# Attention with a mixture of experts on one core: eight of nine expert turns written out with constant counts, one spare block, and the first row numbers loaded ahead of the waits

## The chip, the cores and the metric

The kernel runs on one core of one Trainium2 chip. Its time is the device time of one execution in microseconds. A profile is one further execution under the hardware profiler; its times are read from the start of its span.

## What is computed

One layer: linear attention with a residual, then a mixture of 16 experts of which each token takes two, with a residual. There are 16 x 256 = 4096 tokens of 128 numbers. An expert keeps no more than 640 tokens of each choice; later ones are dropped.

```python
    x = x + _L0_attn_ref(_layernorm(x, axis=-1), L0_attn_W_qkv, L0_attn_W_out, L0_attn_b_out)
    # attention: q = relu(q) + EPS; k = relu(k) + EPS; kv = k^T v; z = 1 / (q . sum(k) + EPS)
    #            out = (q kv z) W_out^T + b_out, by batch of 256 tokens
    # experts:
    logits = xf @ router_w
    probs = jax.nn.softmax(logits, axis=-1)
    w, idx = lax.top_k(probs, K)                       # K = 2 of E = 16
    ...
    keep = myrank < capacity                           # 640
    ...
    gate = jnp.einsum('ecd,edh->ech', xe, gate_w)
    up = jnp.einsum('ecd,edh->ech', xe, up_w)
    hidden = jax.nn.silu(gate) * up
    out = jnp.einsum('ech,ehd->ecd', hidden, down_w)
    out = out * wbuf[:, :, None]
    combined = jnp.zeros((T + 1, D), dtype=xf.dtype).at[dispatch.reshape(-1)].add(out.reshape(-1, D))
```

## The kernel before, in words

The program is written by hand for five engines, with a semaphore for every hand-over. It has three phases.

**Attention phase.** 16 steps, one for a batch of 256 tokens, each cut into stages that run with a lag against each other. For each step POOL takes a power (L350) for the layer norm and then issues four indirect DMAs (L366): each scatters 128 token rows (128 numbers, the expert's mark and the token's number, 528 bytes) from `xf` into the HBM buffer `xbuf` (in the profile: expert_rows), where each expert has a region of `PITCH` rows. The last three steps have no power before their scatters, since the powers run three steps ahead of the routing. At the start SP writes `SPARES` = 14 blocks of empty rows behind the experts' regions (L286), then zeroes `y2` (in the profile: expert_results). At the end of the phase SP, ACT and POOL write a block of empty rows (`tailrows`) behind each expert's last row (`write_tails`: seven, seven and two), and DVE and PE work out three tables: how many turns there will be (`turns_i`), the row at which each block begins (`row_i`), and each block's expert (`exp_i`, `eblk`).

**Expert phase.** A block is 128 rows of one expert. A turn is `U` = 8 blocks. The number of turns is known only on the chip; in the profiled execution it is 9, so 72 blocks. Each block goes through the engines so: SP loads its rows into `xe` (L305); PE transposes them (L922), ACT copies the result to `xeT` (L485); DVE copies the expert's weights to `ew` (L770) and makes the rows' targets `dst` (L780); PE multiplies gate and up (L931), ACT takes silu (L491), DVE the product `hT` (L787), PE multiplies down (L940), ACT copies to `ye` (L499), and POOL scatters the rows of `ye` into `y2` by an indirect DMA (L392). `xe`, `ew`, `ye` and `dst` have eight buffers each, so a buffer is used again one turn later; `xeT`, `sg`, `hT` have two.

PE, DVE and SP have turn 0 written out and ACT turns 0 and 1; the turns behind are a loop on each engine (`Fori`), POOL's loop has all of them. In a loop the counts to wait for are registers, worked out anew each turn (`counts_of`, `done_of`, L253), and a wait for a register's value stands beside an increment of a dummy semaphore `b_held`. At the start of each turn SP and DVE load the turn's eight row numbers and expert numbers into registers (`table_of`, L245). SP's order at the start of the phase: wait for `rows`, load `turns`, wait for the spares, all tails and all scatters (`d_spare`, `d_tail`, `d_ptail`, `d_sc`), load eight row numbers, issue eight loads of `xe`.

**Final phase.** When POOL's last scatter has landed (`d_ye`, then `y_all`), SP and ACT load the results (`yg`), DVE, ACT and POOL weight them and add them to `xa`, and SP writes the output.

The names and lines that the change touches are `sizes` (L7), SP's `load_turn` (L298), POOL's loop (L386), ACT's (L516), DVE's `turn` (L790) with `row_i` (L759), and PE's loop (L949).

Of the kernel before, what the change touches and what calls it, by code (L numbers as in the profile page):

```python
# [6 lines left out]
def sizes(tokens, experts, choices):  # L7

    cap = -(-tokens * choices * 5 // (experts * 4))
    blk = 128  # L10
    maxb = -(-choices * cap // blk)
    pitch = maxb * blk + blk
    per_turn = 8
    minturns = 3


    spares = max(per_turn - 1, minturns * per_turn - choices * cap // blk)
    return cap, blk, maxb, pitch, per_turn, minturns, spares


def linear_attention_moe(nc, x, w_qkv, w_out, b_out, router_w, gate_w, up_w, down_w,
# [13 lines left out]
    P = 128  # L35
# [5 lines left out]
    CAP, BLK, MAXB, PITCH, U, MINTURNS, SPARES = sizes(NB * N, E, K)  # L41
    SPARE = E * PITCH
    DROPPED = SPARE + SPARES * BLK
    MAXN = K * NB * N // BLK + E
    MAXN += -MAXN % U
    NTOK = NB * N
    W = D + 4
# [6 lines left out]
    with ExitStack() as ctx:  # L54
# [141 lines left out]
        NS = 4  # L196
# [45 lines left out]
        def table_of(eng, tab, i, last):  # L242

            at = tab[0:1, U * i:U * i + U] if isinstance(i, int) else tab[0:1, bass.ds(U * i, U)]
            return nc.values_load_multi_w_load_instructions(  # L245
                at, engines=[eng.engine], min_val=0, max_val=last,
                skip_runtime_bounds_check_because="DVE makes the table from the experts' numbers and PITCH")[1]
# [23 lines left out]
        def _(sp):  # L271
# [18 lines left out]
            sp.wait_ge(T["rows"], 1)  # L290
            turns = sp.value_load(turns_i[0:1, 0:1], min_val=0, max_val=MAXN // U - MINTURNS) + MINTURNS
            sp.wait_ge(d_spare, 16 * SPARES)
            sp.wait_ge(d_tail, 16 * POOLT)
# [3 lines left out]

            def load_turn(i, counts):  # L298
                rows = table_of(sp, row_i, i, DROPPED - BLK)
                for u in range(U):  # L300
                    done_of(sp, "xeT_ps", counts, u, U)
                    if not isinstance(i, int):
                        sp.sem_inc(b_held, 1)
                    done_of(sp, "dst", counts, u, U)
                    sp.dma_start(xe[:, u, :], xbuf[bass.ds(rows[u], BLK), :]).then_inc(d_xe[u], 16)  # L305

            load_turn(0, counts_of(sp, 0))
            with sp.Fori(1, turns) as i:
                load_turn(i, counts_of(sp, i, range(-U // NS, 0)))

# [10 lines left out]
        def _(pool):  # L321
# [63 lines left out]

            with pool.Fori(0, turns) as i:  # L386
                counts = counts_of(pool, i, range(U // NS))
                for u in range(U):

                    done_of(pool, "ye", counts, u, 0)  # L390
                    pool.sem_inc(b_held, 1)
                    nc.gpsimd.indirect_dma_start(  # L392
                        out=y2, out_offset=bass.IndirectOffsetOnAxis(ap=dst[:, u:u + 1], axis=0),
                        in_=ye[:, u, :], in_offset=None,
                        bounds_check=K * NTOK - 1, oob_is_err=False).then_inc(d_ye[u], 16)
            for u in range(U):
                pool.wait_ge(d_ye[u], 16 * turns)
                pool.sem_inc(b_held, 1)
# [10 lines left out]
        def _(act):  # L409
# [105 lines left out]
            turn(counts_of(act, 1), 16, None)  # L515
            with act.Fori(2, turns) as i:  # L516
                turn(counts_of(act, i), act.snap(16 * i), act.snap(16 * i - 16))
# [17 lines left out]
        def _(dve):  # L535
# [222 lines left out]
            dve.wait_ge(T["rows_ps"], 1)  # L758
            nc.vector.tensor_copy(row_i[:, :], banks[5][0:1, P:2 * P]).then_inc(T["rows"], 1)  # L759
            nc.vector.tensor_copy(exp_i[:, :], banks[5][0:1, 0:P])  # L760
# [29 lines left out]
            def turn(i, counts, landed, scattered):  # L790
                experts = table_of(dve, exp_i, i, E)
                of_turn = eblk[:, 0:U] if isinstance(i, int) else eblk[:, bass.ds(U * i, U)]
                nc.vector.tensor_copy(eturn[:, :], of_turn).then_inc(b_eturn, 1)
                for u in range(U):
                    weights(counts, u, experts[u])
                    if u == 0:
                        dve.wait_ge(b_eturn, i + 1)
                        dve.sem_inc(b_held, 1)
                    targets(counts, u, landed, scattered)
                    if u >= 1 or not isinstance(i, int):  # L800
                        hidden(counts, u)

            dve.wait_ge(d_ew, 48)
            turn(0, counts_of(dve, 0), 16, None)
            with dve.Fori(1, turns) as i:
                turn(i, counts_of(dve, i, range(-U // NS, U // NS)), dve.snap(16 * i + 16), dve.snap(16 * i))
# [13 lines left out]
        def _(pe):  # L820
# [122 lines left out]
            for u in range(U):  # L943
# [3 lines left out]
                if u >= 2:  # L947
                    down(counts, u)
            with pe.Fori(1, turns) as i:  # L949
                counts, landed = counts_of(pe, i), pe.snap(16 * i + 16)  # L950
                for u in range(U):
                    transpose_in(counts, u, landed)
                    gate_up(counts, u)
                    down(counts, u)
            last = counts_of(pe, turns, range(-1, 0))
            gate_up(last, 0)
# [32 lines left out]
```

## Time and profile before

| | us |
|---|---|
| median of three runs without a profile | 262.67 |
| lowest and highest | 262.15, 263.38 |
| span of the profiled execution | 303.2 |
| attention phase's scatters in it, first to last start | 37.8 to 140.3 |
| expert phase's scatters in it, first to last start | 152.3 to 272.8 |

The profiled execution has no time of its own beside its span. The span runs from the first instruction recorded to the last, and is 40.5 us longer than the median of the runs that carry no profile. So a duration of one instruction can be taken from it, but a stretch of the span cannot be set equal to a stretch of the timed run without asking what the waits in it are. In the rows, the first two columns of a time line or a chain are the start and the duration in us; brackets hold the engine's idle time before the instruction and what ended it; a row of a source line gives count, durations in ns (least, median, most) and the first and last start.

### The profile page before, as it was taken

Reading aid. Unit: us, or ns where it says so; the run is one execution under the profiler, and the core shown is the slowest. Engines: PE = TensorE matmul, PEld = TensorE weight load, DVE = VectorE, ACT = ScalarE, POOL = GpSimd, SP = SyncE. Lnnn points to the kernel's source line nnn. Section 1 sums busy time; section 2 is a strip of 40 time slices with the busy share of each in tenths; the row PEclk is TensorE's granted clock in tenths of the full one; section 3 lists DMA queues with packets and bytes.
Section 4 is the critical chain, followed back from the end, with each engine's and each line's share of the span. In section 5 each row is a group of like instructions: output and inputs, shape, how many; then the busy total and the mean of one; then the engine's idle time right before and its main releaser. Section 6 shows DMA issues by size and latency. Waiting matters only on the chain.

```text
span 303.2 us, 5241 instructions
## 1 busy us (share of the span) xinstructions
PE 181.9 (60%) x1016; PEld 153.2 (51%) x1016; DVE 172.2 (57%) x985; ACT 126.0 (42%) x448; POOL 174.4 (58%) x200
## 2 busy tenths in 40 slices
PE   6684969877764765401569585866877576640000
PEld 5574848666553754301458474755766465530000
DVE  5987766567485657762345364454546354510892
ACT  2663865557574643220244233443435333420330
POOL 4775388585758757866056565556565565651360
PEclk9588995688999795555596879598779897965555
DMA  7997941010101111115332222222232222105992
GB/s 212 294 287 220 291 151 50 27 53 28 47 31 51 37 38 37 54 55 170 81 99 80 74 74 74 67 69 78 67 88 79 64 81 61 40 27 151 290 318 81
DMA packets 46148, 31.62 MB, mean 104 GB/s; under 512 B 4589, under 2 KB 42483, under 8 KB 46130
## 3 DMA queue, kind: packets, MB, share of 16 engines
q1 hardware_dynamic: 36482, 20.20, 25.0%
q0 software_dynamic: 4416, 8.67, 8.5%
q10 hardware_dynamic: 5232, 2.57, 3.3%
q14 instruction: 13, 0.11, 0.1%
q8 instruction: 5, 0.08, 0.1%
HBM read 14.57 MB, written 17.36 MB: 105 GB/s over the span
## 4 chain that ended last, share of the span: by engine, by line
issue 42%; PE 18%; another core or an unknown queue 13%; SPq 10%; DMA 5%; ACT 4%; DVE 4%; ACTq 1%; POOL 0%; POOLq 0%; DVEq 0%
PE bank L931 12%; PE bank L940 4%; DMA yg<-expert_results 3%; SPq L286 3%; PE bank L922 2%; ACT xeT L485 2%; DVE ysum L267 2%; DVE xa L267 2%; ACT ye L499 1%; SPq L240 1%; SPq L281 1%; SPq L280 1%; SPq L278 1%; ACT sg L491 1%
## 5 line engine op out<-in xcount | busy, mean ns | idle before, releaser
L392 POOL DMA_INDIRECT expert_results<-ye,dst x72 | 70.5, 979 | 60.8 <-ACT ye L499 39.7
L366 POOL DMA_INDIRECT expert_rows<-xf,slots x64 | 63.4, 990 | 25.0 <-issue 17.4
L931 PE MATMUL bank<-xeT,ew 128*128 128x128 f32 x288 | 57.6, 333 | 13.7 <-ACT xeT L485 9.9
L931 PEld LDWEIGHTS bank<-xeT,ew 128*128 128x128 f32 x288 | 47.8, 236 | 20.1 <-ACT xeT L485 13.1
L940 PE MATMUL bank<-ew,hT 128*128 128x128 f32 x144 | 37.7, 350 | 20.3 <-issue 14.4
L787 DVE TENSOR_TENSOR hT<-sg,bank 128x128 f32<-128x128 f32 x72 | 20.6, 286 | 51.4 <-ACT sg L491 32.7
L491 ACT ACTIVATE sg<-bank 128x128 f32<-128x128 f32 x72 | 20.1, 279 | 48.8 <-remote 23.3
L940 PEld LDWEIGHTS bank<-ew,hT 128*128 128x128 f32 x144 | 27.0, 234 | 25.0 <-issue 16.8
L499 ACT ACTIVATE ye<-bank 128x128 f32<-128x128 f32 x72 | 20.1, 280 | 22.1 <-remote 15.1
L770 DVE COPY ew<-ew_sb 128x384 f32 x72 | 27.9, 387 | 1.3 <-issue 1.3
L922 PE MATMUL bank<-ident,xe 128*128 128x128 f32 x72 | 23.5, 327 | 7.4 <-DMA xe<-expert_rows 7.1
L485 ACT ACTIVATE xeT<-bank 128x128 f32<-128x128 f32 x72 | 20.1, 280 | 18.4 <-PE bank L922 16.5
L350 POOL TENSOR_TENSOR rs<-ve,minus_half 128x2 f32<-128x2 f32 x16 | 12.2, 763 | 13.8 <-DVE ve L617 13.6
L848 PE MATMUL bank<-ident,xf 128*128 128x128 f32 x32 | 8.7, 366 | 18.0 <-ACT xf L452 16.8
L888 PE MATMUL bank<-gs,qk 128*128 128x129 f32 x64 | 12.6, 326 | 8.1 <-ACT gs L419 5.8
L922 PEld LDWEIGHTS bank<-ident,xe 128*128 128x128 f32 x72 | 12.2, 170 | 9.2 <-DMA xe<-expert_rows 7.7
L452 ACT ACTIVATE xf<-xa,nb,rs 128x128 f32<-128x128 f32 x32 | 13.9, 484 | 4.4 <-DVE nb L579 4.4
L888 PEld LDWEIGHTS bank<-gs,qk 128*128 128x128 f32 x64 | 9.7, 217 | 11.2 <-ACT gs L419 8.0
L267 DVE SCALAR_TENSOR_TENSOR ysum<-yg,wts,xa 128x128 f32<-128x128 f32 x24 | 9.3, 421 | 10.5 <-DMA yg<-expert_results 10.5
L419 ACT ACTIVATE gs<-bank 128x129 f32<-128x129 f32 (+1 forms) x32 | 8.7, 273 | 14.7 <-remote 8.0
L848 PEld LDWEIGHTS bank<-ident,xf 128*128 128x128 f32 x32 | 4.5, 176 | 20.4 <-ACT xf L452 18.9
L860 PE MATMUL bank<-wkT,xnT 128*128 128x128 f32 x64 | 14.2, 359 | 0.7 <-ACT xnT L419 0.7
(140 smaller groups left out, 400.1 us busy)
## 6 DMA issues: line engine op xcount, KB each, us to landing
xe<-expert_rows SPq DMA_DIRECT2D x72, 66.0 KB
expert_results<-zeros SPq DMA_DIRECT2D x1, 4096.0 KB
xs<-in_L_attn_x_dram SPq DMA_DIRECT2D x4, 512.0 KB, 5.3
yg<-expert_results SPq DMA_DIRECT2D x8, 256.0 KB, 8.6
yg<-expert_results ACTq DMA_DIRECT2D x8, 256.0 KB, 9.8
out_dram<-xa SPq DMA_DIRECT2D x8, 256.0 KB, 4.9
expert_rows<-tailrows SPq DMA_DIRECT2D x21, 66.0 KB, 3.3
expert_results<-ye,dst POOLq DMA_INDIRECT x72
```

The source lines that it names most:

```text
L267: nc.vector.scalar_tensor_tensor(out=(ysum if k == 0 else xa)[:, j, :], in0=yg[:, k, j, :], scalar=wts[:, j, k:k + 1], in1=(xa if k == 0 e ...
L366: nc.gpsimd.indirect_dma_start(out=xbuf, out_offset=bass.IndirectOffsetOnAxis(ap=slots[:, col:col + 1], axis=0), in_=xf[:, g % R, j, :], i ...
L392: nc.gpsimd.indirect_dma_start(out=y2, out_offset=bass.IndirectOffsetOnAxis(ap=dst[:, u:u + 1], axis=0), in_=ye[:, u, :], in_offset=None, ...
L485: nc.scalar.activation(xeT[:, u % 2, :], banks[u % 2][:, 0:P], ACT.Copy).then_inc(B["xeT"][u % NS], 1)
L491: nc.scalar.activation(sg[:, v % 2, :], banks[2 + v % 2][:, 0:P], ACT.Silu).then_inc(B["sg"][v % NS], 1)
L499: nc.scalar.activation(ye[:, v, :], banks[4 + v % 2][:, 0:D], ACT.Copy).then_inc(B["ye"][v % NS], 1)
L770: nc.vector.tensor_copy(ew[:, u, :], ew_sb[:, bass.ds(e, 1), :].rearrange("p o h -> p (o h)")).then_inc(B["ew"][u % NS], 1)
L787: nc.vector.tensor_tensor(hT[:, v % 2, :], sg[:, v % 2, :], banks[2 + v % 2][:, P:2 * P], ALU.mult).then_inc(B["hT"][v % NS], 1)
L888: ins = mm(banks[4][:, j * (D + 1):(j + 1) * (D + 1)], qk[:, q % R, j * P:(j + 1) * P], gs[:, q % R, D:], start=True, stop=True)
L922: nc.tensor.transpose(banks[u % 2][:, 0:P], xe[:, u, 0:D], ident[:, :]).then_inc(B["xeT_ps"][u % NS], 1)
L931: ins = mm(banks[2 + v % 2][:, c * P:(c + 1) * P], ew[:, v, c * D:(c + 1) * D], xeT[:, v % 2, :], start=True, stop=True)
L940: mm(banks[4 + v % 2][:, 0:D], hT[:, v % 2, :], ew[:, v, 2 * D:], start=True, stop=True).then_inc(B["y_ps"][v % NS], 1)
```

## The change

Every engine now has turns 0 to 7 written out (`STATIC` = 8), with constants in its waits, and a loop for the turns from 8 on. `MINTURNS`, the least number of turns, becomes 4096 x 2 / 1024 + 1 = 9. `b_held` is incremented in loops only. One spare block is written in place of 14; row numbers of blocks past the last one are cut to `SPARE` by a minimum in the instruction that fills `row_i`, so all such blocks read that one. SP's register load of turn 0's row numbers moves ahead of its waits.

```diff
-    minturns = 3
-    spares = max(per_turn - 1, minturns * per_turn - choices * cap // blk)
+    minturns = choices * tokens // (blk * per_turn) + 1
+    spares = 1
...
+    STATIC = MINTURNS - 1
...
             turns = sp.value_load(turns_i[0:1, 0:1], min_val=0, max_val=MAXN // U - MINTURNS) + MINTURNS
+            rows0 = table_of(sp, row_i, 0, DROPPED - BLK)
             sp.wait_ge(d_spare, 16 * SPARES)
...
-            def load_turn(i, counts):
-                rows = table_of(sp, row_i, i, DROPPED - BLK)
+            def load_turn(i, counts, rows):
...
-            load_turn(0, counts_of(sp, 0))
-            with sp.Fori(1, turns) as i:
-                load_turn(i, counts_of(sp, i, range(-U // NS, 0)))
+            load_turn(0, counts_of(sp, 0), rows0)
+            for i in range(1, STATIC):
+                load_turn(i, counts_of(sp, i), table_of(sp, row_i, i, DROPPED - BLK))
+            with sp.Fori(STATIC, turns) as i:
+                load_turn(i, counts_of(sp, i, range(-U // NS, 0)), table_of(sp, row_i, i, DROPPED - BLK))
...
-            with pool.Fori(0, turns) as i:
-                counts = counts_of(pool, i, range(U // NS))
+            def scatter_turn(i, counts):
                 for u in range(U):
 
                     done_of(pool, "ye", counts, u, 0)
-                    pool.sem_inc(b_held, 1)
+                    if not isinstance(i, int):
+                        pool.sem_inc(b_held, 1)
...
+            for i in range(STATIC):
+                scatter_turn(i, counts_of(pool, i))
+            with pool.Fori(STATIC, turns) as i:
+                scatter_turn(i, counts_of(pool, i, range(U // NS)))
...
-            nc.vector.tensor_copy(row_i[:, :], banks[5][0:1, P:2 * P]).then_inc(T["rows"], 1)
+            nc.vector.tensor_scalar(row_i[:, :], banks[5][0:1, P:2 * P], float(SPARE), None, ALU.min).then_inc(T["rows"], 1)
...
-                        dve.sem_inc(b_held, 1)
+                        if not isinstance(i, int):
+                            dve.sem_inc(b_held, 1)
...
-            with dve.Fori(1, turns) as i:
+            for i in range(1, STATIC):
+                turn(i, counts_of(dve, i), 16 * i + 16, 16 * i)
+            with dve.Fori(STATIC, turns) as i:
...
+            for i in range(1, STATIC):
+                turn(counts_of(pe, i), 16 * i + 16)
+            with pe.Fori(STATIC, turns) as i:
+                turn(counts_of(pe, i), pe.snap(16 * i + 16))
```

ACT's loop is changed in the same way as PE's, with turns 2 to 7 written out behind the two that it had.

On SP, at the start of the expert phase, the order before is this (ISA rows are register instructions, `d_` semaphores count DMAs that have landed):

```order
L291 TENSOR_LOAD turns_i [waits t_rows]
L291 ISA x2
L245 TENSOR_LOAD row_i [waits d_sc2,d_sc1,d_sc3,d_sc0,d_sc4,d_ptail,d_sc5,d_tail,d_spare]
L305 ISA
L305 DMA xe<-expert_rows 128x132
L305 ISA
```

At the same place of the changed kernel, whose lines in this part have numbers one lower:

```order
L290 TENSOR_LOAD turns_i [waits t_rows]
L290 ISA x2
L244 TENSOR_LOAD row_i
L304 ISA [waits d_sc2,d_sc1,d_sc3,d_sc0,d_sc4,d_ptail,d_sc5,d_tail,d_spare]
L304 DMA xe<-expert_rows 128x132
L304 ISA
```

The register load of `row_i` has moved ahead of the nine waits.

On POOL, the whole expert phase before is one loop, entered by a branch and left by a compare:

```order
L386 UNCONDITIONAL_BRANCH [waits d_zero]
L386 ISA
L392 DMA expert_results<-ye,dst 8192x128 [waits b_ye0]
L392 DMA expert_results<-ye,dst 8192x128 [waits b_ye1]
L392 DMA expert_results<-ye,dst 8192x128 [waits b_ye2]
L392 DMA expert_results<-ye,dst 8192x128 [waits b_ye3]
L253 REGISTER_ALU
L392 DMA expert_results<-ye,dst 8192x128 [waits b_ye0]
```

In the changed kernel the phase begins with 64 scatters with nothing between them:

```order
L384 ISA x2
L393 DMA expert_results<-ye,dst 8192x128 [waits b_ye0,d_zero]
L393 DMA expert_results<-ye,dst 8192x128 [waits b_ye1]
L393 DMA expert_results<-ye,dst 8192x128 [waits b_ye2]
L393 DMA expert_results<-ye,dst 8192x128 [waits b_ye3]
L393 DMA expert_results<-ye,dst 8192x128 [waits b_ye0]
```

The branch and the register instructions have gone from between the scatters of a turn and of two turns.

On DVE, at the boundary from turn 0 to turn 1, before:

```order
L805 UNCONDITIONAL_BRANCH
L805 ISA
L245 TENSOR_LOAD exp_i
L793 REGISTER_ALU
L793 COPY eturn<-eblk 128x8
L253 ISA
L770 ISA [waits b_y_ps0]
L770 COPY ew<-ew_sb 128x384
L797 REGISTER_ALU
L774 ISA [waits b_eturn]
```

And in the changed kernel:

```order
L244 TENSOR_LOAD exp_i
L801 COPY eturn<-eblk 128x8
L778 ISA [waits b_y_ps0]
L778 COPY ew<-ew_sb 128x384
L783 TENSOR_TENSOR second<-xe,eturn 128x1 [waits d_xe0,b_eturn]
```

The register load of the eight experts' numbers has stayed; the branch and the arithmetic on registers around it have gone.

## Rows read from the trace of the kernel before

**Rows 1.** The page: its span and POOL's busy time.

```profile
span 303.2 us, 5241 instructions
...
PE 181.9 (60%) x1016; PEld 153.2 (51%) x1016; DVE 172.2 (57%) x985; ACT 126.0 (42%) x448; POOL 174.4 (58%) x200
```

**Rows 2.** Time line of POOL in the attention phase.

```profile
119.73 1.04 POOL L366 DMA_INDIRECT expert_rows<-xf,slots  x1 [0.19 <-issue]
...
123.62 0.97 POOL L366 DMA_INDIRECT expert_rows<-xf,slots  x1 [0.30 <-issue]
...
125.54 1.03 POOL L366 DMA_INDIRECT expert_rows<-xf,slots  x1 [0.19 <-issue]
```

**Rows 3.** Time line of POOL in the expert loop, blocks 31 and 32.

```profile
205.92 0.97 POOL L392 DMA_INDIRECT expert_results<-ye,dst  x1 [0.30 <-issue]
207.20 0.97 POOL L392 DMA_INDIRECT expert_results<-ye,dst  x1 [0.31 <-issue]
```

**Rows 4.** Who waited for whom: us in total, times, longest us.

```profile
POOL expert_results L392 <- ACT ye L499: 39.7, 16, 9.8
...
DVE sel L678 <- remote: 9.3, 5, 2.1
```

**Rows 5.** Time line of ACT in the expert loop.

```profile
201.98 0.28 ACT L491 ACTIVATE sg<-bank 128x128 f32<-128x128 f32 x1 [2.30 <-remote]
...
204.76 0.28 ACT L491 ACTIVATE sg<-bank 128x128 f32<-128x128 f32 x1 [0.29 <-PE bank L931]
...
205.59 0.28 ACT L491 ACTIVATE sg<-bank 128x128 f32<-128x128 f32 x1
```

**Rows 6.** Source lines 366 and 392: POOL's scatters of both phases.

```profile
L366 POOL DMA_INDIRECT expert_rows<-xf,slots x64: 969/974/1199, 37.8 to 140.3; - x64
...
L392 POOL DMA_INDIRECT expert_results<-ye,dst x72: 971/973/1112, 152.3 to 272.8; - x72
```

**Rows 7.** Source line 386: the end of POOL's loop.

```profile
L386 POOLq COMPARE_BRANCH  x9: 40/45/58, 163.0 to 272.4; - x9
```

**Rows 8.** Time lines of PE and DVE at turn boundaries.

```profile
212.52 1.06 PE L931 MATMUL bank<-xeT,ew 128*128 128x128 f32 x4
...
214.01 1.06 PE L931 MATMUL bank<-xeT,ew 128*128 128x128 f32 x4
...
215.94 0.79 PE L931 MATMUL bank<-xeT,ew 128*128 128x128 f32 x4 [0.23 <-issue]
...
200.05 0.17 DVE L793 COPY eturn<-eblk 128x8 f32 x1 [0.71 <-issue]
```

**Rows 9.** Stretch of the loop: us, engines' busy time, granted clock, DMA.

```profile
161.80:272.80 111.00, 77.74 (x443) 66.29 (x442) 53.94 (x257) 43.50 (x191) 63.47 (x65) 0.82 0.24 69
```

**Rows 10.** The chain of waits where the expert phase starts.

```profile
143.32 1.60 DMA expert_rows<-tailrows
...
144.99 0.53 SPq L245
...
145.70 0.37 SPq L305
...
146.26 1.87 DMA xe<-expert_rows
```

**Rows 11.** Time line of DVE: the cast of the row numbers.

```profile
140.66 0.28 DVE L759 CAST row_i<-bank 1x128 int32<-1x128 f32 x1 [1.41 <-issue]
```

**Rows 12.** Source line 286: issue of the spare blocks' writes.

```profile
L286 SPq DMA_DIRECT2D expert_rows<-tailrows x14: 424/432/3472, 15.2 to 24.4; - x14
```

**Rows 13.** DMA queues: packets, MB, share; the page, then 180 to 290 us alone.

```profile
q14 instruction: 13, 0.11, 0.1%
...
q1 hardware_dynamic: 10460, 5.03, 18.5%
q0 software_dynamic: 1824, 3.26, 8.8%
q10 hardware_dynamic: 3771, 1.88, 6.7%
```

More of the change, by code:

```diff
@@ L515, in _ @@
             turn(counts_of(act, 1), 16, None)
-            with act.Fori(2, turns) as i:
+            for i in range(2, STATIC):
+                turn(counts_of(act, i), 16 * i, 16 * i - 16)
+            with act.Fori(STATIC, turns) as i:
                 turn(counts_of(act, i), act.snap(16 * i), act.snap(16 * i - 16))
@@ L791, in turn @@
                 experts = table_of(dve, exp_i, i, E)
-                of_turn = eblk[:, 0:U] if isinstance(i, int) else eblk[:, bass.ds(U * i, U)]
+                of_turn = eblk[:, U * i:U * i + U] if isinstance(i, int) else eblk[:, bass.ds(U * i, U)]
                 nc.vector.tensor_copy(eturn[:, :], of_turn).then_inc(b_eturn, 1)
@@ L797, in turn @@
                         dve.wait_ge(b_eturn, i + 1)
-                        dve.sem_inc(b_held, 1)
+                        if not isinstance(i, int):
+                            dve.sem_inc(b_held, 1)
                     targets(counts, u, landed, scattered)
-                    if u >= 1 or not isinstance(i, int):
+                    if u >= 1 or not isinstance(i, int) or i > 0:
                         hidden(counts, u)
@@ L948, in _, with turn @@
                     down(counts, u)
-            with pe.Fori(1, turns) as i:
-                counts, landed = counts_of(pe, i), pe.snap(16 * i + 16)
+            def turn(counts, landed):
                 for u in range(U):
```

## The prediction, made before the changed kernel was run

> **What bounds the kernel now.** I read the page first. Its span is 303.2 us [rows 1], but the three timed runs, which carry no profile, have a median of 262.67 us. The profiled execution is 40.5 us longer, so the first question is which of its waits the timed runs have. POOL, the engine of the scatters, is busy 58% of the span [rows 1].
>
> The time line of POOL comes next. In the attention phase, where the code is straight and has no loop, a scatter takes 0.97 us and the next starts 0.30 us behind it, without waiting for anything: 1.28 us apart. One step of four scatters and one power takes 5.81 us (119.73 to 125.54) [rows 2]. In the expert loop scatters start 1.28 us apart as well, and these two are blocks 31 and 32, the last of one turn and the first of the next [rows 3]: POOL's own branch costs nothing. What breaks the rhythm is a wait for ACT's `ye`: 39.7 us in 16 waits, of which the first, 9.8 us, is the start of the phase [rows 4].
>
> Why is ACT late? In [rows 5] it stands still for 2.30 us with "remote" as the releaser, which is to say nothing that the profile can name, and then runs through a block in 0.83 us (204.76 to 205.59). Such pauses hit the straight code of the attention phase too (9.3 us in 5 waits of DVE [rows 4]). I take them for the price of recording, and test that with a sum. If POOL never waited, the 71 distances between scatters from 152.3 to 272.8 us [rows 6] would take 71 x 1.28 = 90.9 us and not 120.5: 29.6 us less. From the first scatter at 37.8 to the last at 140.3 us [rows 6] there are 13 steps of 5.81 us and, since the last three steps have no power, 11 distances of 1.28: 89.6 us. They took 102.5: 12.9 us less. 303.2 - 29.6 - 12.9 = 260.7 us, against 262.67 timed. So POOL's scatters bound both phases of a timed run, and about 2.0 us are left in which somebody else does.
>
> **The change part by part.** The sum is made against a timed run understood in this way: of the profiled execution's 303.2 us it takes what lies on the path once the 42.5 us of pauses are out.
>
> POOL's turns written out: the register, compare and branch instructions go, and the increment of `b_held`. They lie under the 0.97 us of a scatter, and the straight scatters of [rows 2] have the distance of the looped ones of [rows 3]. Worth 0. If that cover were gone: the branch takes 0.04 us [rows 7], and with the two register instructions beside it a turn has some 0.12 us, 1.0 us in eight.
>
> PE, DVE and ACT written out: a loop's end costs PE and DVE something that POOL doesn't show. In a slow stretch PE starts blocks 1.49 us apart inside a turn (212.52 to 214.01) and 1.93 us apart over the boundary (214.01 to 215.94). DVE sits 0.71 us before `eturn` [rows 8]; most of that is the register load of eight experts' numbers, the like of SP's 0.53 us [rows 10], and it stays, since each written-out turn still has one. I take the gain at 1.93 - 1.49, 0.4 us a boundary, where a producer is the bound, and at nothing where POOL is. POOL takes 8 x 1.28 = 10.2 us for a turn. PE takes 8 x 1.49 + 0.4 = 12.3 us at its slow rate, and some 8 x 0.83 + 0.4 = 7.0 us at the fast rate of [rows 5]. The granted clock is 0.82 from 161.8 to 272.8 us [rows 9], nearer to the full one than to the half; so PE keeps ahead except at the start, where it comes out of an idle stretch. After it, the seven distances between a scatter and the use of its buffer (9.0 us) cover a landing and a block's work. One boundary, at most two, lies on the path: -0.4 us. The bounds are 0 and 8 x 0.4 = -3.2 us.
>
> SP's first register load: in the chain of waits the tails land at 143.32 + 1.60 = 144.92 us, then SP loads eight row numbers for 0.53 us, and the first `xe` load goes out at 145.70 [rows 10]. In the changed kernel the register load stands ahead of the nine waits and needs only `rows`, which DVE has cast by 140.94 us [rows 11]. Behind it on SP are queued the same wait and the same eight loads. Of the 0.78 us between landing and issue, 0.15 to 0.2 us of register instructions stay: -0.6 us. In a timed run SP's seven tails may be out sooner, but POOL's two come behind its last scatter and land later than `rows` is ready, so the load stays hidden. The bounds are 0, if `rows` is last after all, and -0.7 us. All up to POOL's first `ye` comes earlier by it, and POOL is the bound from there.
>
> One spare block in place of 14: 13 writes of 66 KB and their issue on SP go, 0.43 us each, 5.6 us in all, before 25 us [rows 12]. SP's next wait is for the experts' counts, which end with the attention phase, over 100 us later. Worth 0; without that cover it would be the 5.6 us. The zeroing of `y2` starts earlier by them, and only POOL's first scatters, at 37.8 us, could meet it; nobody waits for their landing then. Bounds 0 and -0.3 us.
>
> The minimum in place of the copy of `row_i`, and nine turns at least in place of three, change no duration: 72 blocks run before and after.
>
> Longer code has to be fetched. The page counts 13 instruction packets of 0.11 MB on one queue [rows 13]. The written-out turns add about as much again. I find no stop of POOL's straight scatters that only a fetch explains, and take 0. The bounds: 0, and twice the 1.87 us from issue to landing of an `xe` load [rows 10], if POOL waits twice for its code: +3.7 us.
>
> Sum: 0 - 0.4 - 0.6 + 0 + 0 = -1.0 us, so 262.7 - 1.0 = 261.7 us.
>
> **The branch itself.** Between 180 and 290 us each engine takes its back branch several times (POOL's nine end at 272.4 us [rows 7]), and the DMA view of that stretch lists three queues, none of them an instruction queue [rows 13]: a turn of the loop isn't fetched again. The Trainium skill says of branches in general (Runtime: NRT & Kernel Launch, Instruction fetch mechanics) that one to a target outside the pages held has to wait for a fetch, and that kernels prefer full unrolling for it. By that rule, if it bites here, eight boundaries on each engine would get cheaper by a fetch; by the rows they get none. Rival 2 prices it.
>
> **The rivals.** (1) The producers, and not POOL, bound a timed run all through, and each of eight boundaries costs its 0.4 us. For it: PE's slow rate is slower than POOL, and the 2.0 us that my sum leaves. Against: the sum itself, which has room for 2.0 us and not for more. It gives 262.7 - 0.6 - 3.2 = 258.9 us. (2) A refetch at each back branch. 13 packets took 0.1% of 16 engines' 303.2 us, 0.37 us each [rows 13]; eight on the path give 3.0 us, with the first load 259.1 us. Against: no packet in 110 us. (3) Slower: the straight code isn't there when POOL wants it. POOL runs over a hundred instructions more just once, and so comes into new code once or twice. A stop of 1.87 us at each, less the 1.0 us won, gives 263.6 to 265.4 us. It decides as soon as POOL's stops add up to more than 1.0 us. For it: all five engines will fetch in the phase, where after 180 us none did. Against: 64 straight scatters, with no odd gap but those that all engines share. (4) The first load isn't on the path, and no boundary is: 262.7 us, no change at all.
>
> **How the numbers follow.** My forecast (-1.0 us, its own range 261.0 to 262.4) gets 0.45, rival 4 0.10, rival 1 0.20, rival 2 0.08, rival 3 0.17. A measurement of this kernel can tell 0.5%, 1.3 us, from no change: faster is under 261.4, slower is over 264.0. A quarter of the forecast's chance lies under 261.4; with rivals 1 and 2 that makes 0.39 faster. Of rival 3, 0.13 is over 264.0. The rest, 0.48, is same. The range takes in rival 1 and the lower part of rival 3: 258.9 to 264.2.
>
> **What would show it.** In the profile of the changed kernel: POOL's scatters stay 1.28 us apart inside a turn and over a boundary; SP's load of `row_i` ends before the tails land, with 0.15 to 0.2 us from the landing to the first `xe` issue; PE's blocks over a boundary are no more than 1.5 us apart at the slow rate; instruction packets appear between 150 and 270 us, with no stop of POOL at them. The span may fall by much more than the time, since fewer instructions are recorded; that would be no gain. Wrong would be timed runs under 260 us (producers or fetches were on the path), or gaps of a microsecond on POOL at the instruction packets.

## The result, and the profile after

The changed kernel has a median of 262.06 us over 13 runs (261.32 to 262.77); the kernel before, run beside it, 262.78 us over 13 (261.76 to 264.15). The ratio is 0.9968, with a 95% interval of 0.9953 to 0.9984: 0.7 us less, where 1.0 was forecast. Ratios compare fast executions only, so on the chip of the last four kernels below, whose executions scatter by more than 2%, a ratio does not follow from the medians beside it.

The execution that was profiled took 261.95 us, and its span is 260.1 us. The first lines of the page, and the group of POOL's scatters:

```profile
span 260.1 us, 4927 instructions
...
PE 158.1 (61%) x1016; PEld 133.5 (51%) x1016; DVE 168.1 (65%) x985; ACT 127.0 (49%) x448; POOL 174.0 (67%) x200
...
L393 POOL DMA_INDIRECT expert_results<-ye,dst x72 | 71.0, 987 | 31.1 <-issue 17.1
```

Against [rows 1] the span is 43 us shorter, and POOL is busy for the same 174 us. This is no gain of the change. The kernel before was profiled once more (first experiment below), and its span is then 261.2 us. The 303.2 us of [rows 1] were an execution with pauses, and 260.1 has to be read against 261.2.

The source line of the expert phase's scatters in the changed kernel (durations in ns: least, median, most; then first and last start), which answers to [rows 6]:

```profile
L393 POOL DMA_INDIRECT expert_results<-ye,dst x72: 966/972/1145, 139.5 to 231.2; - x72
```

71 distances in 91.7 us, 1.29 us each. The time line of POOL over a boundary of turns (190.12 is block 39, 191.39 is block 40):

```profile
184.83 0.97 POOL L393 DMA_INDIRECT expert_results<-ye,dst  x1 [0.30 <-ACT ye L505]
186.11 1.15 POOL L393 DMA_INDIRECT expert_results<-ye,dst  x1 [0.31 <-issue]
187.56 0.97 POOL L393 DMA_INDIRECT expert_results<-ye,dst  x1 [0.30 <-issue]
...
190.12 0.97 POOL L393 DMA_INDIRECT expert_results<-ye,dst  x1 [0.30 <-issue]
191.39 0.97 POOL L393 DMA_INDIRECT expert_results<-ye,dst  x1 [0.30 <-issue]
```

The rhythm is that of [rows 3], 1.28 us. What breaks it now and then is a scatter that itself takes 1.15 us; the gap ahead of each stays 0.30 us. Where the bracket names ACT, the block had long been ready: in the first line the block's `ye` is written 5.3 us before POOL takes it. PE, DVE and ACT run ahead of POOL by four blocks and wait for its landings to give buffers back (page, DVE's group of the targets):

```profile
L788 DVE SCALAR_TENSOR_TENSOR dst<-second,xe 128x1 uint32<-128x1 f32 x72 | 12.0, 167 | 25.1 <-DMA expert_results<-ye,dst 23.5
```

The chain of waits where the expert phase starts, which answers to [rows 10]:

```profile
127.90 0.98 POOL expert_rows L367
128.88 0.58 POOL expert_rows L239
129.45 2.85 DMA expert_rows<-tailrows
132.42 0.04 SPq L304
132.57 0.37 SPq L304
...
133.13 2.28 DMA xe<-expert_rows
```

The register load of `row_i` is gone from it. It starts at 127.8 us and takes 0.87, so it has been done for over 3 us when POOL's tail lands at 132.30; the first `xe` load goes out 0.27 us later.

The instruction queues of the page, then of 150 to 230 us alone (packets, MB, share of 16 engines):

```profile
q8 instruction: 9, 0.15, 0.2%
q14 instruction: 19, 0.16, 0.2%
...
q8 instruction: 4, 0.07, 0.3%
q14 instruction: 8, 0.07, 0.3%
```

Twelve packets of code arrive from 150 to 230 us. [rows 13] has none, but its window opens late in the phase; the kernel before, profiled again, has one packet from 150 to 230 us. Over the whole span it is 28 packets against 18.

### The profile page after: what moved, and what is told of

It reads as the page before. It is cut to its first block, busy times and chain, and to the rows that moved or that the text cites. A ratio compares the mean times of both kernels' runs of the same rounds, so it can differ in the third digit from the quotient of the medians.

```text
span 260.1 us, 4927 instructions
## 1 busy us (share of the span) xinstructions
PE 158.1 (61%) x1016; PEld 133.5 (51%) x1016; DVE 168.1 (65%) x985; ACT 127.0 (49%) x448; POOL 174.0 (67%) x200
## 4 chain that ended last, share of the span: by engine, by line
issue 27%; POOL 20%; DMA 18%; DVE 16%; PE 12%; ACT 2%; SPq 1%; POOLq 1%; ACTq 1%; DVEq 0%
POOL expert_rows L367 13%; DMA expert_results<-ye,dst 11%; PE bank L942 5%; PE bank L951 4%; POOL expert_results L393 3%; DMA yg<-expert_results 3%; DVE ysum L266 2%; DMA xs<-in_L_attn_x_dram 2%; DVE xa L266 2%; POOL rs L351 2%; DVE st L569 2%; DVE nb L587 2%; PE bank L933 1%; DMA expert_rows<-tailrows 1%; DVE ve L576 1%
## 5 line engine op out<-in xcount | busy, mean ns | idle before, releaser
L942 PE MATMUL bank<-xeT,ew 128*128 128x128 f32 x288 | 46.6, 286 | 3.6 <-issue 3.6
L942 PEld LDWEIGHTS bank<-xeT,ew 128*128 128x128 f32 x288 | 39.1, 197 | 6.6 <-issue 5.9
L951 PE MATMUL bank<-ew,hT 128*128 128x128 f32 x144 | 33.3, 313 | 13.7 <-DVE hT L795 13.1
L951 PEld LDWEIGHTS bank<-ew,hT 128*128 128x128 f32 x144 | 21.9, 191 | 20.3 <-DVE hT L795 19.2
L788 DVE SCALAR_TENSOR_TENSOR dst<-second,xe 128x1 uint32<-128x1 f32 x72 | 12.0, 167 | 25.1 <-DMA expert_results<-ye,dst 23.5
L778 DVE COPY ew<-ew_sb 128x384 f32 x72 | 27.6, 383 | 0.5 <-issue 0.5
L933 PE MATMUL bank<-ident,xe 128*128 128x128 f32 x72 | 20.4, 283 | 9.8 <-DMA xe<-expert_rows 9.8
L933 PEld LDWEIGHTS bank<-ident,xe 128*128 128x128 f32 x72 | 10.6, 147 | 10.4 <-DMA xe<-expert_rows 10.4
L467 ACT ACTIVATE ex<-lsub 128x32 f32<-128x32 f32 x16 | 3.7, 229 | 24.3 <-DVE lsub L637 24.1
L587 DVE SCALAR_TENSOR_TENSOR nb<-mv,rs 128x2 f32<-128x2 f32 x16 | 6.1, 382 | 14.5 <-POOL rs L351 14.5
L539 ACT ACTIVATE yg<-yg,wts 128x128 f32<-128x128 f32 x16 | 5.2, 391 | 20.5 <-issue 16.3
```

What stands on the lines that cost most here:

```text
L778: nc.vector.tensor_copy(ew[:, u, :], ew_sb[:, bass.ds(e, 1), :].rearrange("p o h -> p (o h)")).then_inc(B["ew"][u % NS], 1)
L933: nc.tensor.transpose(banks[u % 2][:, 0:P], xe[:, u, 0:D], ident[:, :]).then_inc(B["xeT_ps"][u % NS], 1)
L942: ins = mm(banks[2 + v % 2][:, c * P:(c + 1) * P], ew[:, v, c * D:(c + 1) * D], xeT[:, v % 2, :], start=True, stop=True)
L951: mm(banks[4 + v % 2][:, 0:D], hT[:, v % 2, :], ew[:, v, 2 * D:], start=True, stop=True).then_inc(B["y_ps"][v % NS], 1)
```

## Experiments

### The kernel before, profiled again

No edit.

> The kernel before, unchanged, profiled once more. If the pauses of its first profile (ACT waiting 23.3 us for a releaser without a name) are the price of recording and no property of its loops, a second profile may be free of them: a span near 261 us, attention scatters from first to last start in about 89.6 us, expert scatters in about 91 to 92 us, all 1.28 us apart over the turn boundaries. The rival, that the loops themselves cause the pauses and the written-out turns removed them, expects the span near 303 us again with expert scatters taking about 120 us.

It took 262.92 us, with a span of 261.2. Source line of the scatters, then the chain at the start of the expert phase:

```profile
L392 POOL DMA_INDIRECT expert_results<-ye,dst x72: 966/972/1157, 140.0 to 231.4; - x72
```

```profile
128.48 0.59 POOL expert_rows L240
129.07 2.98 DMA expert_rows<-tailrows
132.14 0.04 issue
132.18 0.53 SPq L245
132.75 0.04 SPq L305
132.90 0.37 SPq L305
```

The scatters span 91.4 us where the sum of the prediction had 90.9, and 89.7 us in the attention phase where it had 89.6. The reading that POOL bounds both phases holds. The pauses do not belong to a profile: this one has none. The rival, that the loops cause them, falls too: these are the same loops. From the landing at 132.05 to the first `xe` issue at 132.90 there are 0.84 us, the register load's 0.53 in them.

### The parts of the change apart

Each is one part put on the kernel before, or taken out of the changed one; all on the chip of the experiment above, where the kernel before has 261.44 us (29 runs).

The earlier register load alone:

```diff
+            rows0 = table_of(sp, row_i, 0, DROPPED - BLK)
             sp.wait_ge(d_spare, 16 * SPARES)
...
-            load_turn(0, counts_of(sp, 0))
+            load_turn(0, counts_of(sp, 0), rows0)
```

> The kernel before with only SP's first load of eight row numbers moved ahead of its nine waits; loops and 14 spare blocks stay. My theory gives this step 0.6 us of the 0.7 us that the whole change won: 262.1 to 262.3 us against 262.7 before, ratio 0.997 to 0.999, and in the profile 0.2 to 0.3 us from the landing of POOL's tails to the first xe load. The rival, that the written-out turns won it, expects no change here (ratio 1.000).

The written-out turns alone (the changed kernel with 14 spare blocks and the register load behind the waits):

```diff
-    spares = 1
+    spares = 14
...
-            rows0 = table_of(sp, row_i, 0, DROPPED - BLK)
...
-            load_turn(0, counts_of(sp, 0), rows0)
+            load_turn(0, counts_of(sp, 0), table_of(sp, row_i, 0, DROPPED - BLK))
```

> The changed kernel with SP's load of row numbers back behind the waits and with 14 spare blocks: the written-out turns alone. My theory: 0 to 0.4 us faster than before, ratio 0.998 to 1.001, POOL's expert scatters 1.28 us apart as in loops. The rival that producers bound the phase expects all of the 0.7 us here, ratio 0.997; the rival that straight code has to be waited for expects a ratio over 1.002.

One spare block alone:

```diff
-    spares = max(per_turn - 1, minturns * per_turn - choices * cap // blk)
+    spares = 1
...
-            nc.vector.tensor_copy(row_i[:, :], banks[5][0:1, P:2 * P]).then_inc(T["rows"], 1)
+            nc.vector.tensor_scalar(row_i[:, :], banks[5][0:1, P:2 * P], float(SPARE), None, ALU.min).then_inc(T["rows"], 1)
```

> The kernel before with one spare block in place of 14 and the minimum on the row numbers; loops and the place of the load stay. My theory expects no change (ratio 0.999 to 1.001): SP has over 100 us of room behind these writes. The rival, that the traffic removed in the first 40 us lets the attention phase start sooner, expects up to 0.3 us less and the first scatter of the attention phase earlier.

| kernel | median us | ratio, 95% interval | tail's landing to first `xe` issue, us |
|---|---|---|---|
| load alone | 261.0 | 0.9975, 0.9957 to 0.9992 | 0.27 |
| turns alone | 261.33 | 0.9982, 0.9962 to 1.0002 | 0.85 |
| spare block alone | 261.61 | 0.9998, 0.9977 to 1.0018 | 0.84 |

The load is worth 0.84 - 0.27 = 0.57 us in the trace and 0.44 in the medians. It is the one part that is seen in both. The spare block can't be told from nothing: its interval reaches 0.6 us to one side and 0.5 to the other. Nor can the turns alone, by the time; what they do is read by phases, below.

### Who bounds the expert phase

Four kernels, on a chip where the kernel before has 262.0 us (13 runs). First the changed kernel with work added on a producer, one copy of 128x128 on ACT for each block of the written-out turns:

```diff
+                if isinstance(counts.get(0), int):
+                    act.wait_ge(c_wc, 2 + idle_n[0])
+                    nc.scalar.activation(idle_tile[:, :], zeros[:, :], ACT.Copy).then_inc(c_wc, 1)
+                    idle_n[0] += 1
```

> The changed kernel with one more ACT copy (128 x 128, 0.28 us) for each block of the eight written-out turns, ahead of silu. ACT then works 1.12 us for a block and is still under POOL's 1.28. My theory, POOL bounds the phase and a block's rows are ready over 5 us before POOL takes them: no change against the changed kernel, within 0.3 us of 262 (ratio 0.996 to 0.999 against before). The rival, producers bound the phase: up to 64 x 0.28 = 17.9 us longer.

260.67 us, ratio 0.9958 (0.9937 to 0.9978); the changed kernel itself did not run on this chip, its ratio on its own chip was 0.9968. ACT's line of the added copies:

```profile
L500 ACT ACTIVATE idle_tile<-zeros 128x128 f32<-128x128 f32 x63 | 19.5, 310 | 0.0
```

19.5 us of work more on ACT cost nothing that these ratios show. Then the changed kernel with work added on POOL, a memset ahead of each of the 64 scatters:

```diff
+                    if isinstance(i, int):
+                        pool.wait_ge(c_pool, 12 + idle_n[0])
+                        nc.gpsimd.memset(idle_tile[:, :], 0.0).then_inc(c_pool, 1)
+                        idle_n[0] += 1
```

> The changed kernel with one more POOL memset (128 x 128, 0.15 to 0.20 us) ahead of each scatter of the eight written-out turns. My theory, POOL bounds the phase: 64 times 0.15 to 0.5 us longer, 10 to 30 us. The rival, producers bound it: no change as long as a scatter and its memset stay under the producers' time for a block.

269.32 us, ratio 1.0282 (1.0251 to 1.0314). Time line of POOL:

```profile
199.80 0.23 POOL L394 MEMSET idle_tile<- 128x128 f32 x1
200.19 0.97 POOL L399 DMA_INDIRECT expert_results<-ye,dst  x1 [0.17 <-issue]
201.16 0.23 POOL L394 MEMSET idle_tile<- 128x128 f32 x1
201.55 1.03 POOL L399 DMA_INDIRECT expert_results<-ye,dst  x1 [0.17 <-issue]
```

A memset of 0.23 us moves the next scatter by 0.08 only (1.36 us apart in place of 1.28), since part of it lies in the gap. The phase from first to last scatter grows from 91.7 to 99.4 us and the span from 260.1 to 267.3; in the medians it is 8.7 us more than with ACT's copies. That is less than the 10 to 30 us expected, since the gap hides part of each memset. What is left of a delay on POOL is paid in full, one on ACT not at all.

Then both kernels with scatters of 32 rows in place of 128; the results of the other 96 rows of each block are left out:

```diff
-                        out=y2, out_offset=bass.IndirectOffsetOnAxis(ap=dst[:, u:u + 1], axis=0),
-                        in_=ye[:, u, :], in_offset=None,
+                        out=y2, out_offset=bass.IndirectOffsetOnAxis(ap=dst[0:32, u:u + 1], axis=0),
+                        in_=ye[0:32, u, :], in_offset=None,
```

> The kernel before, with its loops, but each scatter of results takes only the first 32 of a block's 128 rows; the results of the other rows are left out. If POOL's time for a scatter goes with the rows, POOL stops being the bound and the producers' own rate shows: 0.9 to 1.1 us a block and a break at each turn boundary, 72 blocks in 70 to 80 us in place of 91 to 92. If the time of a scatter is the same for 32 rows, nothing changes.

> The changed kernel with the same light scatters (first 32 of 128 rows of each block, the others left out). If POOL is no longer the bound, this run against the light kernel with loops gives what the written-out turns are worth to producers: by my price 0.4 us at each of eight boundaries, 3.2 us, beside the 0.6 us of the earlier load. If scatters of 32 rows are no faster, it differs by the 0.7 us of the full kernels.

Source line of the scatters, of the loops and then of the written-out turns:

```profile
L392 POOL DMA_INDIRECT expert_results<-ye,dst x72: 864/871/991, 139.4 to 223.5; - x72
```

```profile
L393 POOL DMA_INDIRECT expert_results<-ye,dst x72: 863/870/1113, 137.7 to 222.5; - x72
```

A quarter of the rows takes 0.87 us in place of 0.97, so POOL stays the bound, and these two kernels don't show the producers' own rate that they were made to show. The loops run at 254.63 us (ratio 0.972, 0.9689 to 0.9752), the written-out turns at 253.63 (0.9687, 0.9654 to 0.972). The expert phase of the second is 84.8 us and that of the first 84.1: longer, and yet the kernel is 1.0 us faster. Only a table by phases tells where that comes from.

### Phases of eight traces

All in us. "Step" is the distance between POOL's last two groups of adds (its last L404 or L410 start less the one before). The final phase runs from the first load of `yg` to the end of the span.

| kernel | expert scatters, first to last | final phase | in it: to POOL's first add | step |
|---|---|---|---|---|
| before, again (loops) | 91.43 | 27.62 | 9.45 | 1.90 |
| load alone (loops) | 91.23 | 27.47 | 9.25 | 2.11 |
| spare block alone (loops) | 91.20 | 27.83 | 9.02 | 2.53 |
| 32 rows (loops) | 84.06 | 27.54 | 9.09 | 2.13 |
| turns alone (written out) | 91.94 | 27.11 | 9.46 | 1.49 |
| after (written out) | 91.70 | 26.73 | 9.02 | 1.58 |
| ACT's extra copies (written out) | 92.05 | 26.88 | 9.24 | 1.54 |
| 32 rows (written out) | 84.82 | 26.84 | 9.15 | 1.54 |

The final phase less the last two columns is 16.1 to 16.3 us in all eight rows. So all that tells loops from written-out turns there is the step: 2.2 us on average against 1.5. The table leaves out what comes ahead of the expert phase: its first scatter starts between 137.7 and 140.2 us in the eight traces. That spread of 2.5 us is larger than the differences read here, and each kernel has one trace. The time lines of POOL at the end, of the kernel before (again) and of the changed one:

```profile
250.18 0.48 POOL L404 TENSOR_TENSOR ysum<-yg,xa 128x128 f32<-128x128 f32 x1 [0.77 <-ACT yg L531]
250.74 0.45 POOL L406 TENSOR_TENSOR xa<-yg,ysum 128x128 f32<-128x128 f32 x1
252.08 0.62 POOL L404 TENSOR_TENSOR ysum<-yg,xa 128x128 f32<-128x128 f32 x1 [0.89 <-ACT yg L531]
252.78 0.45 POOL L406 TENSOR_TENSOR xa<-yg,ysum 128x128 f32<-128x128 f32 x1
```

```profile
249.56 0.48 POOL L410 TENSOR_TENSOR ysum<-yg,xa 128x128 f32<-128x128 f32 x1 [0.76 <-ACT yg L539]
250.12 0.45 POOL L412 TENSOR_TENSOR xa<-yg,ysum 128x128 f32<-128x128 f32 x1
251.14 0.45 POOL L410 TENSOR_TENSOR ysum<-yg,xa 128x128 f32<-128x128 f32 x1 [0.57 <-ACT yg L539]
251.67 0.45 POOL L412 TENSOR_TENSOR xa<-yg,ysum 128x128 f32<-128x128 f32 x1
```

Why does POOL's last add matter, when DVE still adds for 3 us after it? The source line that closes the kernel, of the kernel before (again); the first column of times is the duration in ns, the second the start:

```profile
L54 POOLq DRAIN  x1: 8265/8265/8265, 252.7 to 252.7; - x1
...
L54 SPq DRAIN  x1: 13/13/13, 258.0 to 258.0; - x1
L54 SPq EVENT_SEMAPHORE  x1: 17/17/17, 261.2 to 261.2; - x1
```

POOL closes with an instruction named DRAIN, of 8.27 us, that starts with its last add. It ends at 261.0 us, while SP has been done since 258.0. In all 14 traces the DRAIN takes 8.26 to 8.27 us and the span ends 8.5 us after its start. The end of this kernel is set by POOL's last add.

And why is that add later with loops? The DMA view of the final phase has one packet of code in every loop kernel of the table and none in any written-out one. Here the kernel before (again) at 249.1 to 249.8 us, the middle of the last loads of `yg`:

```profile
q1 hardware_dynamic: 235, 0.11, 61.9%
q10 hardware_dynamic: 184, 0.09, 50.5%
q14 instruction: 1, 0.01, 4.0%
```

The engines are full there, and among the rows of `yg` goes a packet of 8 KB of code, which takes 0.45 us (4.0% of 16 engines' 0.7 us). It comes 15.2 to 15.6 us into the final phase. ACT issues its last load of `yg` 6.9 to 7.0 us into the phase in all eight kernels, so that load isn't issued late; it lands late. Among the written-out kernels the one with POOL's extra memsets has a packet in this phase too, at 2.8 us, ahead of the last groups, and its step is 1.49.

### Is it the packet, and is it the DRAIN?

The last four kernels ran on a chip where the kernel before itself takes 303.08 us (298.0 to 363.73, 23 runs), so they are read by the lengths of their undisturbed phases, and their ratios tell little. In their expert phases POOL is not the bound all the time: 32 to 35 of the 72 scatters start less than 1.2 us after ACT began their `ye`, where it is 1 to 3 in the traces of kernels with full scatters that have no pauses.

To move the packet: the kernel with the earlier load alone, with 32 writes of one column each on DVE, put between the expert loop and the final adds.

```diff
+            for k in range(32):
+                nc.vector.memset(shift[:, k:k + 1], 0.0)
```

> The kernel before with the earlier load of row numbers, and 32 one-column memsets on DVE between its last product and its final adds, where it waits for POOL anyway. They only move DVE's later code by 32 instructions. In the kernels with loops one instruction packet goes out 15.5 us into the final phase and the last group of results lands 1.9 to 2.5 us after the group before it; in the written-out ones there is no such packet and it lands 1.5 us after. If the packet is DVE's code and it is the packet that holds up the last group, it now goes out 6 us or more earlier or before the phase, the last group lands 1.5 us behind the one before, POOL's last add and the end come 0.5 us earlier: ratio 0.995 to 0.997 against before. If the packet belongs to another engine, it stays at 15.5 us and the ratio is that of the earlier load alone, 0.9975.

302.67 us (ratio 1.004, 0.997 to 1.011). DMA views of the shifted kernel, 268.8 to 269.8 us, where the last scatter is still under way, and then 272 to 299.3, the whole final phase:

```profile
q0 software_dynamic: 32, 0.07, 20.3%
q14 instruction: 1, 0.01, 2.4%
...
q1 hardware_dynamic: 8448, 4.20, 57.1%
q10 hardware_dynamic: 4224, 2.10, 31.0%
```

The packet has moved ahead of the final phase, so it is DVE's code. The step is 1.67 us and the final phase 27.14, where the same kernel without the shift has 2.11 and 27.47 on another chip. That is half to three quarters of the way to the written-out kernels; a step of 1.5 was expected, and the times, with an interval of 1.4%, can't show a gain of 0.5 us. It is one trace, and another weakens it: the last kernel of this section (loops, same chip) has the packet at 15.5 us, and yet ACT's last load of `yg` lands only 1.73 us behind the one before, against 1.67 in the shifted kernel and 1.58 and 1.47 in the two written-out ones of this chip. Over all 14 traces this distance is 1.73 to 2.53 us in the six with a packet 15.2 to 16.1 us into the phase, and 1.47 to 1.67 in the eight without. The two go together; that the packet makes the whole of the longer step is not shown, and its own 0.45 us don't cover the 1.0 us of the widest case.

To take POOL's last add away: the changed kernel, with the last of POOL's eight tiles given to DVE.

```diff
-            return j % G == G - 1
+            return j % G == G - 1 and j < NT - 1
```

> The changed kernel with the last of POOL's eight token tiles in the final phase (tile 31) given to DVE. POOL's last add ends 18.7 us into the phase and the drain of POOL behind it takes 8.27 us, while SP's last output has landed at 24.0 us. If POOL's drain sets the end, POOL begins it 1.6 to 2.1 us earlier and SP's output, which DVE makes 0.5 us later, takes over at 24.8 to 25.3 us: 1.5 to 1.9 us less, ratio against before near 0.990. The rival, that the drain ends with the outputs whatever POOL does, expects 0.5 us more.

299.28 us (ratio 0.9871, 0.9824 to 0.9918). Its closing source line:

```profile
L53 POOLq DRAIN  x1: 8266/8266/8266, 290.6 to 290.6; - x1
...
L53 SPq DRAIN  x1: 13/13/13, 298.1 to 298.1; - x1
L53 SPq EVENT_SEMAPHORE  x1: 17/17/17, 299.0 to 299.0; - x1
```

POOL's DRAIN starts 16.7 us into the final phase in place of 18.2, and the phase takes 25.2 us in place of 26.7: the 1.5 us are gained in full, and SP and POOL now end within a microsecond of each other. The DRAIN did set the end; at 290.6 + 8.27 = 298.9 us it still does.

The last two add 14 products of zeros on PE ahead of the first block, to raise its clock; one on this kernel, one on the kernel before with the earlier load and the same final phase.

```diff
+            for _ in range(14):
+                mm(banks[7][:, 0:D], zeros[:, :], zeros[:, :], start=True, stop=True)
```

> As final_early, and with 14 matmuls of zeros on PE while it waits for the expert phase's first rows. PE starts that phase at its slow rate (the first blocks 1.49 us apart, the first ye 5.7 us behind the first load). If the matmuls bring it up to the fast rate by then, the first scatter comes 1.0 to 1.5 us earlier and all behind it: ratio 0.985 to 0.987 against before. If they don't, it is that of final_early.

> The same two edits and the earlier load on the kernel before, with its loops and 14 spare blocks. It tells once more what the written-out turns are worth, now without the final phase's luck in them, since POOL's drain no longer ends the span: my theory says that they gain nothing and cost up to 0.5 us, so this one is as fast as the written-out one or 0.5 us faster. A rival that the written-out turns speed up the producers expects it 0.4 us or more slower.

The first took 297.76 us, the second 300.21 (ratio 0.994, 0.9898 to 0.9983). Time lines of PE, the first kernel and then the second:

```profile
142.98 6.24 PE L931 MATMUL bank<-zeros 128*128 128x128 f32 x28 [1.23 <-issue]
149.05 0.38 PE L936 MATMUL bank<-ident,xe 128*128 128x128 f32 x2
```

```profile
141.58 4.84 PE L920 MATMUL bank<-zeros 128*128 128x128 f32 x28 [1.23 <-issue]
146.78 0.33 PE L925 MATMUL bank<-ident,xe 128*128 128x128 f32 x1 [0.36 <-DMA xe<-expert_rows]
```

In the second the zeros end just before the first rows are there, and from 147 us on the granted clock is 1.00, the full level, where the shifted kernel above has 0.50, the half level, up to 150 us and 0.63 on average up to 154; from the first `xe` issue to the first scatter it takes 5.66 us, against 6.63 there. In the first the zeros are still running when the rows arrive, and the same stretch takes 7.94 us, so its first scatter came no earlier, where 1.0 to 1.5 us were expected. So some 1.0 us can be had at the start of the phase, by one trace, if the zeros end in time.

The comparison of the two was also to say what the written-out turns are worth once POOL's last add no longer ends the span, and it came out against the expectation: the loops were to be as fast or 0.5 us faster, and they are 2.4 us slower in the medians, as the rival had it (written-out turns speed up the producers). On this chip, where POOL often waits for the producers, that may be so. The traces don't settle it: from first to last scatter the loops take 119.2 us here and the written-out turns 116.6, but in the other pair of this chip it is 117.4 with loops (shifted) and 119.0 written out (POOL's tile moved). For a time without pauses the phases table stands. Whether the changed kernel with POOL's last tile moved, and with zeros that end in time, is 2 us faster than without them when there are no pauses was not measured.

## Why the prediction was nearly right, step by step

**The sum without the pauses held; the cause given for them did not.** "The price of recording" fell. The kernel before has a span of 261.2 us under the same profiler, and on the chip of the last four kernels runs without any profile take 303 us. The span is 1.7 to 1.9 us shorter than the execution's own time in every kernel here, with pauses or without. That difference is also what the sum of the prediction took for 2.0 us "in which somebody else does": it set 260.7 us of a span against 262.67 us of times, which are 1.7 to 1.9 us more for the same execution. Of the 2.0 us, 0.1 to 0.3 are left, and the argument for rival 1 that rested on them falls. It held to leave 42.5 us out of the sum since the timed runs of 262.67 us have no pauses, not since a profile adds them. They have something of a period: in the trace of the early final phase POOL's scatters at 204.89, 211.82, 218.78 and 225.71 us each come after a wait of 2.1 us. The first of these begins on ACT, which waits 1.89 us ahead of silu for a releaser without a name, while POOL's scatter at 201.79 us runs through it. What the cause is stays open.

**POOL bounds both phases.** Right, as long as there are no pauses. The extra work on POOL was paid in full, that on ACT not at all, and lighter scatters shortened the kernel with loops by 7.4 us.

**SP's register load, -0.6.** Right: 0.84 to 0.27 us, which is 0.57, in both kernels that have the edit. The part that stays is 0.27 and not 0.15 to 0.2.

**The producers' boundary, -0.4.** Wrong. The step that failed is "one boundary, at most two, lies on the path". I took PE's slow rate for the start of the phase, but that rate lasts for the first three or four blocks only, and the start gives them a lead: in the kernel before (again) the `ye` of block 1 is begun 1.15 us before its scatter, that of block 7 2.8 us. POOL's second scatter comes after 0.3 to 0.45 us, the later ones after 0.30. Over boundaries its scatters are 1.28 us apart in the loops. Nor do loops cost PE 0.4 us there: its transposes of blocks 7 and 8 start 0.95 us apart in the loops and 0.91 written out. Without pauses this term is 0, and with it rival 1.

**Code fetch, 0.** Near 0 in sum with the final phase's term below, but not 0 in its parts. No scatter of POOL waits longer at the packets: the gap stays 0.30 us. The expert phase is 91.9 us on average in the three written-out kernels with full scatters and 91.3 in the three with loops, so 0.6 us longer, and 0.8 in the pair with 32 rows. It lies in the scatters' own durations and not in the gaps: with full scatters, 16 of them take over 1.1 us in the three written-out kernels and 7 in the three with loops. That the packets cause them was not shown; only 2 of the 16 have one within them. The prediction counted the 13 packets of one queue and left out the 5 of 16 KB on the other, which changes no term that it summed. Rival 3, a stop at each, did not come.

**A term that the prediction doesn't have.** The final phase is 0.7 us shorter with written-out turns (26.9 against 27.6). The kernel ends with POOL's DRAIN, and this hangs on the last group of `yg`, which lands sooner there; the packet of code is the candidate for the cause. The sum for the turns is +0.6 - 0.7 = -0.1, and with the register load -0.7, which is what was measured. So the total came from one right term, one term that was wrong and two unforeseen ones that cancel; that -1.0 came as near as it did is in part luck.

**The branch itself.** 0, as forecast: the kernel before (again) has no packet of code between 160 and 230 us, although each engine takes its back branch several times there. The Trainium skill (Runtime: NRT & Kernel Launch, Instruction fetch mechanics) has a branch wait for a fetch when its target lies outside the pages held. The trace agrees, in that these loops never meet the condition, and its advice to unroll bought nothing at the branches.

**What is open.** Why some scatters take 1.15 us in place of 0.97; whether the packet makes the 0.7 us or a part of it, since the shifted kernel won only 0.3 of it (that trace has the pauses, though none falls in its final phase) and one kernel with the packet has nearly as short a step; whether written-out turns help on the chip with the pauses; and what the pauses are.

## What to carry to other kernels

Profile an unchanged kernel twice before reading a term of a microsecond out of one trace, and above all when the span is far from the timed runs: compare span and own time of the same execution. Before writing a loop out, look whether the engine that bounds the phase loses anything at the branch; here that engine had its register work under another instruction's 0.97 us, and the written-out turns alone gained nothing that the times can show. Look at what closes the kernel: an engine with a long DRAIN should get its last work early, which was worth 1.5 us of the final phase here, more than the whole change.

## What the runs showed of the hardware that was not expected

- POOL's DRAIN at the end takes 8.26 to 8.27 us in all 14 traces, and DVE's 0.4 to 0.5 us.
- An indirect DMA of 128 rows holds POOL for 0.97 us, one of 32 rows for 0.87: between these two, most of it doesn't go with the rows. With the 0.30 us gap that is 1.28 us for each, and a memset of 0.23 us between two adds only 0.08.
- One 8 KB packet of code, among loads that fill the DMA engines, goes with a last group that comes 0.4 to 1.0 us later than in the written-out kernels in four traces, and in a fifth 0.15 to 0.26; that it is the cause is not shown.
- The same kernel takes 261 to 263 us on some chips and 303 on another, run after run; a trace of that chip has waits of some 2 us about 7 us apart in the stretch that I read.
